# Two layers of a graph network on one core: the counts of a group leave PSUM through ScalarE as 16-bit integers, and VectorE adds them in 16 bits

## What is computed

```
h   = relu(layernorm(x))
msg = (h[src] + edge_attr) @ Wm.T + bm
agg = segment_sum(msg, dst) / max(deg, 1)
x   = x + layernorm(h + gelu([h, agg] @ Wu.T + bu)) * gamma + beta
h   = relu(layernorm(x))
rst = (1 + eps) * h + segment_sum(h[src], dst)
out = x + relu(rst @ W1 + b1) @ W2 + b2 + h
```

## Time and profile before

| | us |
|---|---|
| median of 3 runs | 526.91 (526.67 to 529.15) |
| the profiled execution, and its span in the trace | 526.39, 524.6 |
| PE busy | 482.8 |
| DVE busy | 283.0 |
| ACT busy | 147.5 |
| POOL busy | 166.8 |
| mean granted TensorE clock, share of full | 0.992 |
| chain that ended last: PE, DVE | 63%, 21% |

### The profile page before, as it was taken

The page is one execution under the profiler, slowest core; times in us unless marked ns, Lnnn a source line. Parts: engine busy times, 40 slices in busy tenths (PEclk is TensorE's granted clock), DMA queues, the critical chain, the costliest instruction groups (busy, mean ns, idle before and its releaser), DMA issues.

```text
span 524.6 us, 8826 instructions
## 1 busy us (share of the span) xinstructions
PE 482.8 (92%) x3003; PEld 277.0 (53%) x3003; DVE 283.0 (54%) x660; ACT 147.5 (28%) x291; POOL 166.8 (32%) x217
## 2 busy tenths in 40 slices
PE   5889999898898988999999999599989999999997
PEld 4446554444444544675665655379944446744442
DVE  6897887888777779645434789983000000011111
ACT  4416644123222223222237245441011122100000
POOL 7323665333322224000023267636994000000000
PEclk9999999999999999999999999799999999999999
DMA  8998998889999999988820111112040000011111
GB/s 299 316 367 301 338 327 292 348 342 361 352 367 358 374 363 390 408 308 315 271 82 2 32 29 41 35 62 100 1 163 0 0 0 1 0 41 40 41 40 35
DMA packets 31115, 98.95 MB, mean 189 GB/s; under 512 B 3577, under 2 KB 3577, under 8 KB 31067
## 3 DMA queue, kind: packets, MB, share of 16 engines
q1 hardware_dynamic: 30458, 97.27, 50.7%
q10 hardware_dynamic: 608, 1.05, 0.7%
HBM read 95.76 MB, written 2.56 MB: 187 GB/s over the span
## 4 chain that ended last, share of the span: by engine, by line
PE 63%; DVE 21%; issue 6%; PEld 6%; DVEq 1%; POOL 1%; DMA 1%; SPq 0%; PEldq 0%; POOLq 0%
PE ps L1260 13%; PE ps L1245 13%; PE ps L1007 9%; PE ps L1048 7%; DVE A L669 5%; PE ps L1105 5%; PE ps L1106 4%; PE ps L1018 4%; PE ps L1194 3%; PEld ps L1171 3%; PE ps L1036 3%; PEld ps L1172 2%; DVE U L893 2%; DVE tt L871 2%; DVE oneS L648 2%
## 5 line engine op out<-in xcount | busy, mean ns | idle before, releaser
L400 POOL TENSOR_TENSOR aggT<-turned_sums,aggT 128x88 f32 x118 | 53.9, 456 | 107.4 <-ACT turned_sums L473 94.4
L1007 PE MATMUL ps<-ea,oneD 128*22 128x256 f32 x1264 | 83.9, 383 | 1.4 <-DVE oneD L640 0.9
L947 DVE TENSOR_TENSOR U<-ps,U 128x512 f32<-128x512 f32 (+1 forms) x10 | 6.9, 692 | 130.8 <-PE ps L1260 130.8
L467 ACT COPY packed_sums<-ps 128x256 f32<-128x256 f32 x79 | 29.4, 372 | 163.9 <-PE ps L1007 163.9
L1245 PE MATMUL ps<-aggT,W1s 128*128 (+1 forms) x192 | 67.4, 513 | 2.2 <-PEq L1239 2.2
L1260 PE MATMUL ps<-W2s,hid 128*128 128x512 f32 (+1 forms) x160 | 68.8, 592 | 0.0
L669 DVE TENSOR_TENSOR A<-ps,A 128x220 f32 x158 | 60.3, 381 | 8.6 <-PE ps L1018 8.0
L1018 PE MATMUL ps<-oneK,oneS 128*128 128x220 bf16 x316 | 42.5, 259 | 14.7 <-DVE oneS L648 13.0
L1245 PEld LDWEIGHTS ps<-aggT,W1s 128*128 128x128 f32 x192 | 36.4, 190 | 33.1 <-issue 33.0
L1007 PEld LDWEIGHTS ps<-ea,oneD 128*22 128x22 f32 x1264 | 30.5, 101 | 41.1 <-issue 23.6
L648 DVE TENSOR_TENSOR oneK<-iotaP,P_key 128x880 bf16<-128x880 bf16 x79 | 51.8, 655 | 0.0
(11 more groups left out here) (139 smaller groups left out, 645.1 us busy)
## 6 DMA issues: line engine op xcount, KB each, us to landing
ea<-in_edge_attr_dram SPq DMA_DIRECT2D x78, 1024.0 KB, 7.6
X<-in_x_dram SPq DMA_DIRECT2D x1, 2304.0 KB
xt<-in_x_dram SPq DMA_DIRECT2D x9, 256.0 KB, 2.7
out_dram<-U SPq DMA_DIRECT2D x9, 256.0 KB
W1s<-in_L_gnn_W_dram SPq DMA_DIRECT2D x1, 2048.0 KB, 7.7
W2s<-in_L_gnn_W_dram SPq DMA_DIRECT2D x1, 2048.0 KB, 8.7
WuN<-in_L_gnn_Wu_dram ACTq DMA_DIRECT2D x1, 1024.0 KB, 5.4
WuN<-in_L_gnn_Wu_dram SPq DMA_DIRECT2D x1, 1024.0 KB, 6.8
```

The source lines that it names most:

```text
L400: nc.gpsimd.tensor_tensor(cols, sums, cols, ALU.add).then_inc(early_step, 1)
L1007: last = T.matmul(to.rearrange("p (c d) -> p c d", c=2), oneD[h][:, g * 2 + j, :], data, start=j == 0, stop=j == 1)
```

## The change

ACT copies both halves of a group's counts, 128 x 440, from PSUM to a 16-bit buffer `counted` in SBUF (two buffers, which lie where `h0t` is written later). DVE adds from `counted`, so that both inputs and the output of the add are 16-bit in SBUF. PE may reuse the bank when the copy is done, not the add. POOL waits for the last add before it writes `h0t`. `stats2` is dropped, and `stats` is used in its place, which makes room.

```
+            def counts_copy(m):
+                act.wait_ge(counts_done, m + 1)
+                if m >= HOTS:
+                    act.wait_ge(add_step, (m - HOTS + 1) * 2)
+                nc.scalar.copy(counted[m % HOTS][:], ps[:, 4 + m % 2, 0:2 * KW]).then_inc(counts_out, 1)
...
                 if 0 < n <= EARLY:
                     turned_copy(n - 1)
+                for m in COUNTS[n]:
+                    counts_copy(m)
...
                 if half == 0:
-                    dve.wait_ge(counts_done, m + 1)
+                    dve.wait_ge(counts_out, m + 1)
                 if m > 0 or half > 0:
                     dve.wait_ge(add_step, m * 2 + half)
-                V.tensor_tensor(cols, ps[:, 4 + m % 2, half * KW:(half + 1) * KW].rearrange("p (h w) -> p h w", w=W), cols, ALU.add).then_inc(add_step, 1)
+                V.tensor_tensor(cols, counted[m % HOTS][:, half * KW:(half + 1) * KW].rearrange("p (h w) -> p h w", w=W), cols, ALU.add).then_inc(add_step, 1)
...
                 if m >= 2:
-                    pe.wait_ge(add_step, (m - 1) * 2)
+                    pe.wait_ge(counts_out, m - 1)
...
                     if c == 0 and q == 0 and f < 2:
-                        pe.wait_ge(add_step, 2 * NG)
+                        pe.wait_ge(counts_out, NG)
...
             pool.wait_ge(late_in, 48)
+            pool.wait_ge(add_step, 2 * NG)
...
-                V.bn_stats(stats2[:, b, :], U[:, b, :]).then_inc(x1_stats, 1)
+                V.bn_stats(stats[:, b, :], U[:, b, :]).then_inc(x1_stats, 1)
```

More of the change, by code:

```diff
@@ L136, in gnn_kernel @@
     assert TB * 2048 <= 5 * SUB * GP * 4
+    counted_at = at[0]
+    counted = [place(f"counted{s}", [P, 2 * KW], U16, counted_at + s * 1024)[0] for s in range(HOTS)]
     h0t = [place(f"h0t{i}", [P, D], F32)[0] for i in range(TB)]
@@ L163, in gnn_kernel @@
     mv, _ = place("mv", [P, NT, 2], F32)
-    stats2, _ = place("stats2", [P, NT, 6], F32)
     mv2, _ = place("mv2", [P, NT, 2], F32)
@@ L192, in gnn_kernel @@
         counts_done = sem("counts_done")
+        counts_out = sem("counts_out")
         counts_zero = sem("counts_zero")
@@ L896, in x1_moments @@
                 dve.wait_ge(x1_ready, b + 1)
-                V.bn_stats(stats2[:, b, :], U[:, b, :]).then_inc(x1_stats, 1)
+                V.bn_stats(stats[:, b, :], U[:, b, :]).then_inc(x1_stats, 1)
             def x1_moments2(b):
                 dve.wait_ge(x1_stats, b + 1)
-                V.bn_aggr(mv2[:, b, :], stats2[:, b, :]).then_inc(x1_aggr, 1)
+                V.bn_aggr(mv2[:, b, :], stats[:, b, :]).then_inc(x1_aggr, 1)
             def x1_variance(b):
```

## The result

| kernel | median us (lowest to highest, runs) | ratio to before, 95% interval |
|---|---|---|
| before, beside the change | 527.22 (526.67 to 529.15, 4) | |
| the change | 536.90 (534.50 to 540.23, 4) | 1.0181 [1.0120, 1.0243] |

The change is slower by 9.7 us. Forecast were +4.8 (531.7, range 526 to 541): the sign is right, the size about half. The profiled execution is the fastest of the four, 534.50, with a span of 532.7: 8.1 more than before.

A forecast was written before the change was run, and what follows sets the result against it. PE time was taken as the bound, with PE and DVE holding each other up at two buffers. Opening +1.5, copy +6.0, blocks -2.45, end -0.25 gave +4.8 us on 526.91: 531.7 us, range 526 to 541.

The forecast's parts named there:

- What bounds it: Group loop: PE time sets the end; PE waits 13.0 us for `oneS`, DVE 8.0 us for counts, at two buffers' depth.
- The adds: DVE's adds into `A`: 16-bit SBUF inputs cut each from 381 to about 268 ns, saving 0.23 us per group.
- What the adds share with GpSimd: Adds with two SBUF inputs meet POOL's adds: a block gains 0.07 us, 35 blocks give -2.45 us.
- The rival that was built on the rule: Every POOL add blocks DVE's adds in full: 0.53 us a block, a loss of 0.30, 545 us; chance 0.06.
- The copy: ACT's copy between counts and add takes 0.53 us, delays each of ten restarts behind `u1` by 0.60: +6.0 us.
- The opening: Up to the first `u1`, seven copies exceed ACT's gaps: +1.5 us, between 0 and +2.8.
- The parts at nothing: PE's wait for the copy, the products' first piece, POOL's new wait, `stats2` and DMA: no cost of their own.
- the end: Loop's end: the last round's lateness hides in a 0.74 us gap at 207.79: -0.25 us, bounds 0 and -0.74.
- Not halved: Rival: DVE's adds into `A` are not halved and a block loses up to 0.22 us; 540 us, chance 0.14.
- POOL rarely hits: Rival: POOL rarely meets DVE's adds, so a block gains the full 0.23 us; -0.8 us, 526.1, chance 0.20.
- The restart does not count: Faster rival: PE has other work at late restarts, the 6.0 us vanish, blocks gain 0.23; 520.4 us, chance 0.14.

The follow-up runs named there:

- experiment 7: A third buffer of `oneK` and `oneS`: kernel before 527.47 us, the change 521.39 us; the change with the add freeing the bank again 532.59 us.
- the quiet change: The change with `Hl` moved to the time of `u1` and GpSimd's adds of turned sums cut to one column of 22: 524.40 us.
- experiment 1: The change with adds reading PSUM again, still behind ScalarE's copy, and PE waiting for the adds again: 536.38 us, +9.4 against the kernel before.
- experiment 3: The change with `counted` as 32-bit floats, keeping copy, waits and two SBUF inputs: 547.14 us, +18.6 against the kernel before.
- the quiet pair: Kernel before and the change, both with `Hl` moved to `u1` and GpSimd's adds cut to one column of 22: 521.81 and 524.40 us.

## Why the prediction was right, and where its sizes were off

**What bounds it.** Right. The two engines hold each other up at a depth of two buffers: three buffers take the counts' wait away, but only once the bank is free as well (experiment 7).

**The adds.** Right in size: 268 ns forecast, 257 at best and 284 as median when nothing meets them; 22-element runs at any node do get the 16-bit rate. The Trainium skill (Vector Engine (DVE) Microarchitecture Reference, 5.1) has it that 4-byte alignment makes no difference there, and the tile `A` agrees: in the edges of the reference 80 of the 157 halves begin at an odd node, and the longest of the 158 adds in the quiet change is 318 ns.

**What the adds share with GpSimd.** This is the step of the sum that failed most. The mechanism was named, but the price per block was made from a short hit, 1.5 x 0.18 us, though the earlier trace rows showed the long one as well: the ten `Hl` were not counted on the adds. A block was to gain 0.07 us and gained 0.02, so the term was -0.8, not -2.45. In runs, the collisions cost the change 3.4 (long) + 3.8 (short: 4.8 less 1.0) = 7.2 us more than they cost the kernel before; each of the two is a difference of four medians and known to some 3 to 4 us, and the `u1` starts give 2.9 for the long ones.

Each hit follows one pattern in the rows: a VectorE operation that starts while GpSimd runs ends at GpSimd's end plus its own duration less 0.13 us, a figure that the five pairs were fitted with. At 57.82 that gives 57.38 + 1.64 + 0.28 - 0.13 = 59.17, and the row ends at 59.19; at 96.02 it gives 97.37 and 97.37; at 140.73 it gives 141.16 and 141.16; the two pairs of the earlier trace rows give 113.28 and 113.28, 73.3 and 73.30 (with 0.41 for `oneS`, 0.6 for `oneK`). The rest of the trace was not used for the fit, and it agrees. In the change, from 55 to 207 us, 83 operations of VectorE with two SBUF inputs (26 adds with the three above, 22 `oneK`, 5 `oneS` and 30 `oneD`, of which an undisturbed one takes 0.25) start while one of GpSimd's runs and has more than 0.15 us to go: 80 of them end within 0.03 us of this sum. The other three are `oneK` that start within 0.02 us of GpSimd's add; there VectorE goes first, and GpSimd's add, 0.34 at its shortest, is the one that stands:

```profile
74.27 0.81 POOL L402 TENSOR_TENSOR aggT<-turned_sums,aggT 128x88 f32 x1 [0.21 <-POOL aggT L402]
74.28 0.60 DVE L659 TENSOR_TENSOR oneK<-iotaP,P_key 128x880 bf16<-128x880 bf16 x1
```

So VectorE stands until GpSimd is done, save 0.13 us. That is the rule of the Trainium skill (SBUF — State Buffer, "Who interferes with whom"), and I was wrong to read the 0.59 us row as speaking against it: that hit was short because GpSimd's add was (0.34). The rival that was built on the rule came out too slow: it priced the hits of a block at 0.53 us and the kernel before at none. Against the undisturbed lengths (284, 600, 410 and 250 ns for add, `oneK`, `oneS` and `oneD`) the means of the change give some 0.34 us a block, 2 x 66 + 59 + 46 + 0.76 x 135 ns, and those of the kernel before 0.17 already.

**The copy.** The mechanism held at all ten restarts (0.55 us later, 0.60 forecast), and its duration (0.527). The sum was small: +1.5 and +6.0 were forecast, and experiment 1 has 9.4. The difference lies in the opening (3.2 there) and in the first round, which became 2.4 us later and not 0.6: by the rows of experiment 1 PE's waits for `oneS` grew by 3.1 - 1.2 = 1.9 us in it, and each stands behind a matrix that `Hl` stretched. The rounds after it took 0.53 each on average. The forecast counted no `Hl` on the one-hot matrices of a shifted VectorE either.

**The opening.** +2.0 at the first `u1`, forecast 1.5 within 0 to 2.8.

**The parts at nothing, the end.** The change of the bank's wait is worth nothing with two buffers by the order of VectorE's program, as forecast (no run tries it), but some 10 us with three. The first piece of the products begins with its first conversion 9.15 us later (207.95 and 217.10), and the span is longer by 8.1; so 1.0 is given back behind it, where 0.25 was forecast, with bounds of 0 and 0.74: the measured value lies outside them, and where it is given back was not traced further.

**Not in the forecast.** Behind the stand at 96 us the granted clock fell. Windows of the change (us, busy of PE, PEld, DVE, ACT and POOL, granted clock, DMA share, GB/s):

```profile
96.00:98.00 2.00, 0.17 (x3) 0.09 (x2) 2.00 (x4) 0.66 (x2) 1.79 (x3) 1.00 1.02 397
98.00:100.00 2.00, 2.00 (x22) 0.91 (x22) 2.00 (x4) 0.72 (x2) 1.37 (x2) 0.77 0.98 365
100.00:102.00 2.00, 1.57 (x10) 0.60 (x12) 2.00 (x7) 0.81 (x3) 0.78 (x2) 0.50 0.86 227
102.00:104.00 2.00, 2.00 (x19) 0.82 (x12) 1.89 (x7) 0.64 (x2) 0.40 (x1) 0.50 1.03 422
```

PE was busy 0.17 of 2 us, and behind that it had 0.50 of full speed (1.2 GHz) until about 106 us (the next two windows have 0.52 and 1.00). In the kernel before and in the change with `Hl` moved the clock is 1.00 from 94 to 106 us. That round made the change 1.5 us later, with `Hl` moved 0.3: some 1.2 us for collision and clock together. What the clock alone took was not tried.

**The sum again**, from the stages: opening 2.0, ten restarts with the first round's `Hl` 7.5 (experiment 1, from its first `u1`, 3.24 late, to its first conversion, 10.75 late), blocks -0.8, the round at 96 us 1.2, the end -1.0: 8.9, beside 8.1 between the spans and 9.7 between the medians. It is an estimate: two of its terms come from other kernels, and the forecast's sign was no luck, but its 4.8 is half of this because the blocks paid back 0.8 and not 2.45, and because the first round and the round at 96 us cost some 3 us that it did not have. Cut the other way, by edits: the copy's wait +9.4, the adds' second SBUF input +9.2, the halving -8.9, the last two with what the clock took.

**The rivals.** "Not halved" was priced at 540 and takes 547 (experiment 3): its mean add is 465 ns (36 to 200 us), 79 over its undisturbed length, where the change has 61 over 284, and the clock fell three times. "POOL rarely hits" is the quiet pair: +2.6 there, forecast -0.8, the copies being larger. "The restart does not count" falls with the ten restarts and experiment 1.

What stays open: how much of the 9.4 us of experiment 1 is the copy's wait and how much `Hl` meeting VectorE at other times. With `Hl` moved in both kernels the first round still costs the change 1.3 us and not 0.6, so `Hl` is not all of it. Nor was it taken apart why the opening is 3.2 us late in experiment 1 and 2.0 in the change.

## What to carry to other kernels

Taking an operand from PSUM to SBUF to get a faster VectorE mode is three changes in one: a copy on the path, a second SBUF input that GpSimd can stop, and a bank that comes free early; price each by its own rows, and look for the longest GpSimd operation nearby, not the mean one. A third buffer was worth nothing here while the next resource of the ring (the PSUM bank) had the old depth, so raise them together. Work of GpSimd that has no deadline belongs where VectorE stands idle: that alone made the kernel before 5.7 us faster.

## What the runs showed of the hardware that was not expected

A VectorE operation with both inputs in SBUF that starts while GpSimd's runs ends at GpSimd's end plus its own duration less 0.13 us (80 of 83 in the change, and the pairs above); when it starts first, it is GpSimd that stands (at 139.34 an `oneS` keeps its 0.41 us, and GpSimd's add that starts at 139.40 takes 0.59, where its shortest take 0.34). An add that reads PSUM was never stretched: in the kernel before 58 of the 158 adds start while a GpSimd operation has more than 0.1 us to go, four of these under an `Hl`, and all 158 take 373 to 394 ns; in experiment 1 it is ten under an `Hl`, and none is over 393. And after PE was busy only 0.17 us of two, its clock was granted at 0.50 until about 106 us although PE was busy again.
